# A four-layer transformer stack on one core: the linear attention's context sums spread between the first batch's queries and gates, GpSimd's maxima over partitions put in other places, two scales computed later

## What is computed

```python
x = x + tanh(g_xattn[0]) * linear_attention(layernorm(x), ctx)   # layer "A" in the plan
x = x + tanh(g_ffn[0])   * ffn_gelu(layernorm(x))                 # "F", width 2048
x = x + tanh(g_xattn[1]) * softmax_readout(layernorm(x), ctx, mask)   # "L"
x = x + tanh(g_ffn[1])   * grouped_experts(layernorm(x))          # "M", "E"
# linear attention, per head of 32:
q = phi(layernorm(x) @ Wq.T); k, v = phi(ctx @ Wk.T), ctx @ Wv.T  # phi(t) = t + 1 if t > 0 else exp(t)
kv_summary = einsum('bhsd,bhse->bhde', k, v); k_sum = k.sum(-2)
out = (q @ kv_summary) / (q @ k_sum) * sigmoid(layernorm(x) @ Wg.T + bg) @ Wo.T
```

## Time and profile before

| | |
|---|---|
| time, median of 3 runs | 1887.24 us (1886.98 to 1889.6) |
| the profiled execution | 1887.19 us, span in the trace 1885.4 us |
| PE busy | 1846.4 us, 98% of the span |
| DVE busy | 995.9 us, 53% |
| ACT busy | 538.6 us, 29% |
| POOL busy | 323.5 us, 17% |

### The profile page before, as it was taken

One profiled execution on the slowest core, in us unless ns is written; L12 is line 12 of the kernel. 1 busy time (PEld: TensorE's weight loads), 2 busy tenths in 40 slices (PEclk: granted clock), 3 DMA queues, 4 the chain that ended last, 5 costly groups with the idle time before them and its releaser, 6 DMA issues.

```text
span 1885.4 us, 24612 instructions
## 1 busy us (share of the span) xinstructions
PE 1846.4 (98%) x9552; PEld 905.6 (48%) x9552; DVE 995.9 (53%) x2036; ACT 538.6 (29%) x801; POOL 323.5 (17%) x299
## 2 busy tenths in 40 slices
PE   8799999999999999999999999999999999999999
PEld 3445554644444444444444444444444444444444
DVE  5676776754554455454436554545445455554422
ACT  3224433312221122122112233233333223333321
POOL 1123322222021120202010011111111111111111
PEclk9899999999999999999999999999999999999999
DMA  5124433333414223340310200101010101000000
GB/s 159 55 62 129 140 118 95 96 129 65 104 42 127 90 68 104 70 125 27 90 54 9 76 1 23 32 1 54 1 54 1 54 1 54 1 23 1 1 23 23
DMA packets 135830, 112.10 MB, mean 59 GB/s; under 512 B 75554, under 2 KB 92066, under 8 KB 135714
## 3 DMA queue, kind: packets, MB, share of 16 engines
q1 hardware_dynamic: 135714, 110.53, 19.7%
HBM read 78.00 MB, written 32.51 MB: 59 GB/s over the span
## 4 chain that ended last, share of the span: by engine, by line
PE 83%; issue 9%; DVE 3%; POOL 2%; DMA 2%; ACT 1%; POOLq 0%; SPq 0%; DVEq 0%; ACTq 0%
PE bank L923 44%; PE bank L1012 17%; PE bank L1092 10%; PE bank L992 4%; PE bank L932 3%; PE bank L977 1%; POOL arena L897 1%; PE bank L958 1%; PE bank L1079 1%; PE bank L1027 1%; POOL arena L871 0%; PE bank L1054 0%; DVE arena L1278 0%; DMA arena<-in_L_xattn_Wkv 0%; DMA arena<-x_after_ffn 0%
## 5 line engine op out<-in xcount | busy, mean ns | idle before, releaser
L923 PE MATMUL bank<-arena 128*128 128x512 f16 x4608 | 1042.2, 380 | 8.4 <-DVE arena L1299 7.3
L923 PEld LDWEIGHTS bank<-arena 128*128 128x128 f16 x4608 | 451.1, 98 | 538.9 <-DVE arena L1299 7.8
L1012 PE MATMUL bank<-arena 128*128 128x512 f16 x1536 | 352.1, 379 | 1.2 <-DVE arena L1506 1.2
L1092 PE MATMUL bank<-arena 128*128 128x512 f16 x1152 | 264.3, 379 | 0.9 <-POOL arena L897 0.9
L1648 DVE SCALAR_TENSOR_TENSOR arena<-bank,arena 128x512 f32<-128x512 f32 x96 | 72.0, 750 | 329.0 <-PE bank L923 329.0
L1191 ACT ACTIVATE arena<-bank,arena 128x512 f32<-128x512 f32 x128 | 99.5, 778 | 493.5 <-PE bank L923 490.5
L1012 PEld LDWEIGHTS bank<-arena 128*128 128x128 f16 x1536 | 150.1, 98 | 181.1 <-DVE arena L1506 1.7
L897 POOL TENSOR_TENSOR arena<-arena 128x512 f16<-128x512 f32 x96 | 111.0, 1157 | 626.0 <-ACT arena L1228 626.0
L1504 DVE TENSOR_SCALAR arena<-arena 128x512 f16<-128x512 f32 x128 | 65.8, 514 | 281.6 <-ACT arena L1191 281.3
L1092 PEld LDWEIGHTS bank<-arena 128*128 128x128 f16 x1152 | 112.0, 98 | 128.4 <-POOL arena L897 1.4
L1506 DVE SCALAR_TENSOR_TENSOR arena<-arena 128x512 f16<-128x512 f32 x128 | 118.0, 922 | 4.6
(11 more groups left out here) (159 smaller groups left out, 1215.8 us busy)
## 6 DMA issues: line engine op xcount, KB each, us to landing
arena<-in_L_ffn_proj SPq DMA_DIRECT2D x64, 256.0 KB, 2.9
arena<-in_L_ffn_gate_up_proj SPq DMA_DIRECT2D x96, 96.0 KB, 2.0
x_after_attention<-arena SPq DMA_DIRECT2D x8, 1024.0 KB, 5.2
arena<-x_after_attention SPq DMA_DIRECT2D x8, 1024.0 KB, 5.6
x_after_ffn<-arena SPq DMA_DIRECT2D x8, 1024.0 KB, 4.3
arena<-x_after_ffn SPq DMA_DIRECT2D x8, 1024.0 KB, 6.2
arena<-in_x SPq DMA_DIRECT2D x7, 1024.0 KB, 5.5
normalised_blocks<-arena SPq DMA_DIRECT2D x28, 256.0 KB, 2.0
```

The source lines that it names most:

```text
L923: m = e.matmul(bank[b][:, :], wT[l][:, c, tile * P:(tile + 1) * P], y[h][:, c, :], start=n == 0, stop=n == NPASS - 1)
L1012: m = e.matmul(bank[t][:, :], hv[h][:, 0, t * P:(t + 1) * P], w2T[l][:, j, :], start=j == 0 and i == 0, stop=j == NH - 1 and i == 2)
L1092: m = e.matmul(bank[t][:, :], hv[h][:, 0, t * P:(t + 1) * P], dnT[l][:, j, :], start=j == 0 and i == 0, stop=j == NR - 1 and i == 2)
```

## The change

The sums `kvsum` and the products `numden` of batch 0 are written between the tiles of `q 0` and `gate 0`; the norm of batch 1 begins earlier. The maximum over the partitions of v (`all v`) is written behind the first tile of `q 0`. `tables`, `ctxmax` and the maxima `b1` and `c` move from ahead of `q 1 0` to behind `out 0 0`, and `pow c` behind `out 0 2`. `hscale` is no longer written with `half`, but for "2" at the end of layer A's stage and for "d" before the last part of layer F's. The instructions themselves stay what they were, but their lines are 8 higher in the changed kernel (L856 becomes L864).

```diff
         if name in ("2", "d"):
             add("half", name)
-            late.append(lambda: add("hscale", name))
...
     add("xload", "A", 1)
+    norms = ln_tasks(("A", 1), apart=True)
     for j in range(NC):
         add("q", 0, j, banks=1)
         if j == 0:
             add("keysv", 3)
+            add("vmax")
+            add("all", "v")
             add("pow", "g")
             split("g")
+        else:
+            add("kvsum", j - 1, banks=4)
         flush()
+        if j == 2:
+            add("consts")
+            add("pow", "v")
+        if j > 1:
+            norm(2)
     scaled.update("qg")
-    add("consts")
     add("xload", "A", 2)
-    norms = ln_tasks(("A", 1), apart=True)
     for j in range(NC):
         add("gate", 0, j, banks=1)
-        norm()
         if j == 0:
-            add("vmax")
-            add("all", "v")
-        if j == 2:
-            add("pow", "v")
+            add("kvsum", 3, banks=4)
+        else:
+            add("numden", 0, j - 1, banks=2)
+        if j < 2:
+            norm()
         weights(N_O)
-    for t in range(4):
-        add("kvsum", t, banks=4)
-        if t < 2:
-            norm()
-    for t in range(NT):
-        norm()
-        add("numden", 0, t, banks=2)
-        weights(N_O)
-    add("tables")
-    add("all", "b1")
-    add("ctxmax")
-    add("all", "c")
-    late.append(lambda: add("pow", "c"))
+    norm()
+    add("numden", 0, NT - 1, banks=2)
+    norm(3)
+    weights(N_O)
+    weights(N_O)
...
             add("out", b - 1, t, banks=1)
+            if b == 1 and t == 0:
+                add("tables")
+                add("all", "b1")
+                add("ctxmax")
+                add("all", "c")
+            if b == 1 and t == 2:
+                add("pow", "c")
...
     add("b2")
     weights_until(N_B)
+    add("hscale", "2")
...
                     weights_until(N_D)
+                    add("hscale", "d")
```

## The result

The changed kernel takes 1892.19 us (median of 10 runs, 1889.31 to 1894.71), the kernel before, on the same chip, 1887.78 us (10 runs, 1886.98 to 1889.6). The ratio is 1.0021, 95% interval 1.0012 to 1.0031: slower by some 4.4 us, where 1887.4 with a range up to 1891.5 was forecast. The profiled execution of the changed kernel took 1890.71 us, span 1888.9 us, 3.5 us more than that of before. That one execution lies inside the forecast's range; the median, 1.5 us higher, lies 0.7 us outside it. The changed kernel's runs also scatter twice as far (5.4 against 2.6 us).

The account below looks back on a forecast made before the run. The prediction took TensorE, busy 98% of the span, as the bound, so only its waits and slow stretches counted. Terms -7.1 + 6.0 + 1.3 = +0.2 on 1887.19 us gave 1887.4 us, range 1881.5 to 1891.5.

Parts of the forecast that it names:

- SP's queue issues the same transfers, weights two places later, long before their use: On SP's DMA queue: the later place of the weight loads was taken to cost nothing.
- At no cost: Items counted as free: `hscale d`, two weight tiles split one or two steps later, and SP's queue order.
- `hscale 2`, first half: Near 290 us: VectorE no longer waits for GpSimd's root, so TensorE's 4.3 us wait and 2.8 slow stretch go; -7.1.
- `hscale 2`, second half: Start of layer F: small instructions queue behind GpSimd's additions; TensorE's wait grows 3.7, slow stretch 2.3; +6.0.
- all but the reciprocal are held: Start of layer F: by the shared-port rule, GpSimd's additions hold all the moved `hscale` instructions except the reciprocal.
- its signs: Layer F: L1384 or L1400 near 1 us would support the forecast; small instructions at 0.2 us each would refute it.
- Batch 0: Sums between queries and gates: GpSimd's second addition at 66.5, TensorE stands 10.3 us, `q 1` starts at 94.3; +1.8.
- Batch 1 and the tables: Batch 2's norm ready about 117, -3.9 at `out 0 0`; tables make TensorE wait 3.3 and run slow at `q 2`, together +5.2.
- The maximum of weight 1: Phase of the moved tables: asked for before GpSimd can pass over, it takes VectorE's slack but about 0.2 of TensorE.
- the bound of 3.6 for the tables: First tile of `q 2`: TensorE's wait if none of VectorE's 2.84 us end slack can be used; 3.0 otherwise.
- Nearly free: Rival: one-element instructions slip between the additions (+1.4), clock stays up at `q 2`; 1881.1 us, chance 0.20.
- Dearer passages: Rival: GpSimd's pair of passages costs more, from 17 us between first and second addition; 1892.4 us, chance 0.16.

Follow-up runs that it names:

- e1: Changed kernel with the load of batch 5's x moved behind the load of weight tile 44 on SP's queue; 1888.41 us, ratio 1.0002 to before.
- e9: Changed kernel with the weight steps where they stood before, from `q 1 1` on; 1883.74 us, ratio 0.9972 to before.
- e5: Kernel before with `hscale 2` alone moved, ahead of the last four output tiles of layer A; 1882.47 us, ratio 0.9971.
- e4: Kernel before with the change's two `hscale` moves alone; 1887.01 us, ratio 0.9996.
- e12: Changed kernel with the product at L1400 written with one tensor input instead of two; one run, 1888.98 us, beside 1889.39 before.
- e2: Changed kernel with `hscale 2` ahead of the last four output tiles of layer A instead of behind the second bias; 1887.72 us, ratio 0.9997.
- e3: Changed kernel with the maximum of v moved behind `q 0 3` and `pow v` ahead of the first product; 1883.10 us, ratio 0.9969.
- e11: e10 with the weight steps' schedule restored as in e9 in place of the moved load of x; 1867.82 us, ratio 0.9887.
- e6: Changed kernel with the edits of e1, e2 and e3 together; 1874.47 us, ratio 0.9930.
- e8: e6 with the second bias behind the second of the last four output tiles and batch 1's norm one gate tile earlier; 1871.14 us, ratio 0.9911.
- e10: e8 with the context's maximum two output tiles later and `pow c` behind `q 2 3`; 1869.70 us, ratio 0.9903.
- e7: e6 with the tables and the maxima of b1 and the context back ahead of `q 1 0`, `pow c` behind it; 1878.50 us, ratio 0.9948.

## Why the prediction was wrong

- **"SP's queue issues the same transfers, weights two places later, long before their use" is the step that failed.** It stood under "At no cost" and was not worked out for any tile. Two places later put the load of tile 44 behind a load that waits for a store, and its use came in the next step but one: +6.6 us in the profiled run. e1 takes 5.1 of them away by one place on SP's queue, e9 all of them. Without the stretch the profiled run would be at 1884.1 us. It hid behind an error the other way: against the forecast's +0.2 the profiled run stands at +3.5, made up of +5.8 from `q 3 0` to `out 3 3` (6.6, less 0.8 that the same shift gave back), -3.5 at layer F, where +6.0 was forecast and +2.5 came, +0.5 of later start, and 0.5 of small ones. That this run is inside the range is luck.
- **`hscale 2`, first half (-7.1):** right, -7.0 between `out 3 3` and `q 6 0`. e5 confirms it by 5.7 us of time.
- **`hscale 2`, second half (+6.0):** mis-sized. The wait grew by 2.5, not 3.7, since L1384 and L1406 ran in 0.15 and 0.21 us beside the additions; only the two-input L1400 (1.07) and the tile's own L1512 (0.94) and L1514 were held. L1401 of the earlier trace rows was a bad nearest row. It was held, though it has one tensor input: in the changed kernel the same instruction (L1409, at 57.61 us) meets no addition and takes 0.16 instead of 0.72 us. But it has four elements, and the one-input instructions of one element, L1384 and L1406, were not held. The clock's part was 0 in the changed kernel's profiled run and 2.55 in e4, where the term comes to 5.1. The Trainium skill, "SBUF — State Buffer", section "SBUF: two separate sides", names the instruction "with two SBUF inputs" as one that takes the shared ports; e12 agrees, 0.21 for 1.07 us. That rule does not say that L1384 and L1406 are held unless they run in a two-port mode, which I had taken for given: "all but the reciprocal are held" read more into it than it says. Of its signs, L1400 came near 1 us, but L1384 and L1406 ran in the 0.2 us that were to refute it.
- **Batch 0 (+1.8):** right. The second addition came at 66.86 (66.5 forecast), TensorE stood 3.49 and 7.70 us (2.7 and 10.3), `q 1 0` started at 94.57 (94.3), 0.53 of it a later start of the whole program. That TensorE stood 2.6 us less than forecast changes nothing: it came later (61.2, not 58.3), and the relu sets the end (68.94; forecast 68.6).
- **Batch 1 and the tables (-3.9 and +5.2):** the wait at 118 to 122 went to 0.27 us, the one at `q 2 0` was 2.64 (3.3 forecast) with 4.13 us for its slow tile. The maximum of weight 1 cost more than 0.2: its passage took 7.35 instead of 6.39 us, L1262 waited 5.92, and with TensorE's small gaps behind it batches 0 and 1 stood at +1.9 at `q 3 0` (0.5 of it the later start) where +1.3 was forecast. That this is near is partly luck: up to `q 2 0` they had come 0.8 us better than forecast, and from there to `q 3 0` they lost 1.0 where 0.2 was forecast, which e9 shows to be the weight steps again. The norm of batch 2 was there at 119.8 and not at "about 117": it just met TensorE. And the bound of 3.6 for the tables does not follow from its rows: 5.1 and 0.75, less the slack of 2.84, are 3.0, without the slack 5.85.
- **The rivals.** "Nearly free" was nearer at layer F (+1.4; +2.5 came, with the clock up, two of the small instructions not held and one held), wrong at `q 2`, where the clock fell, and wrong in the time, because of the same missing term. "Dearer passages" was not the cause: 13.8 us between the two additions, far from its 17; that its 1892.4 us is the measured time is luck. The loss came from none of the cases; the list of what could go wrong had no case for SP.

## What to carry to other kernels

Where a step is dropped from a planner that paces itself, every later step of it moves; print the order of the DMA queue on both sides and look at each place where a load has crossed a transfer that waits. A queue in order makes a transfer's cost depend on what stands ahead of it, not only on its length. An instruction that is moved off one stall needs a place that is checked like the one it left: half a stage earlier `hscale 2` was free, beside GpSimd's additions it gave up to three quarters of its gain back.

## What the hardware showed that I had not expected

- The same wait is paid once in some kernels and twice in others. Behind 2.60 to 2.65 us at `q 2 0` the tile took 4.1 to 4.5 us in the changed kernel, e1, e2, e3, e9, e11 and e12, and 2.76 or 2.77 in e6, e8 and e10. Behind 3.7 to 3.8 us at layer F it took 2.76 in the changed kernel and 4.2 to 5.3 in e3, e4 and e9. Behind the waits of 4.99 us (e5), 5.57 (e4) and 7.68 (e7) ahead of `out 0 0` the tile was slow each time (5.15, 4.86 and 5.14 us). What decides it for the short waits stays open here. The number of such waits does not tell how far a kernel's times scatter either: 5.4 us between the runs of the changed kernel, 1.1 between those of e5, though e5's trace has waits of 3.16, 2.64 and 4.99 us.
- The start of the program varies by itself: the relu of `q 0 0`, which no edit touches, came between 44.06 and 45.86 us. Compare stretches, not starts.
- GpSimd's passage from the ordinary kind to the maximum, where no semaphore releases it, took 5.69 (e5) to 7.93 us (e3) in these traces, back 6.68 (e2) to 7.82.
